# Extra node tiles and the lead of the pairs spread over the run, and the last sum moved ahead, in a graph layer on one core

## What is computed

```python
src = node_feature[edge_src]
parts = [jax.nn.relu(node_feature)]
for t in range(n_types):
    msg = jax.nn.relu(src @ W_e[t].T + b_e[t])
    msg = jnp.where((edge_type == t)[:, None], msg, jnp.zeros((), msg.dtype))
    parts.append(jax.ops.segment_sum(msg, edge_dst, num_segments=N))
agg = jnp.concatenate(parts, axis=1)
for t in range(n_types):
    o = agg @ W_n[t].T + b_n[t]
    updated = jnp.where((node_type == t)[:, None], o, updated)
# result: layernorm(x + updated + x)
```

## Time and profile before

| | us |
|---|---|
| median of three runs | 907.19 |
| profiled execution, whole | 908.36 |
| its span, first to last instruction | 906.6 |
| GpSimd busy | 674.5 (74%) |
| TensorE busy | 717.5 (79%) |
| VectorE busy | 614.0 (68%) |
| ScalarE busy | 145.8 (16%) |

### The profile page before, as it was taken

The page is one execution under the profiler, slowest core; times in us unless marked ns, Lnnn a source line. Parts: engine busy times, 40 slices in busy tenths (PEclk is TensorE's granted clock), DMA queues, the critical chain, the costliest instruction groups (busy, mean ns, idle before and its releaser), DMA issues.

```text
span 906.6 us, 13972 instructions
## 1 busy us (share of the span) xinstructions
PE 717.5 (79%) x4555; PEld 601.7 (66%) x4555; DVE 614.0 (68%) x1468; ACT 145.8 (16%) x397; POOL 674.5 (74%) x718
## 2 busy tenths in 40 slices
PE   5593066896998888888888889889887798889796
PEld 3362065785877776676677777778666677778674
DVE  6999988467676557556656666665765476757756
ACT  3293100111111101101111010111111011112120
POOL 7777777777777777777777777777777777777771
PEclk9796558799999989999999999989999898989999
DMA  8495532343543344333443344335335533434321
GB/s 251 145 313 154 138 96 77 97 111 51 146 118 105 97 109 106 96 110 90 99 122 92 94 105 113 94 94 123 95 96 128 146 69 103 110 77 121 81 53 50
DMA packets 71985, 101.39 MB, mean 112 GB/s; under 512 B 18057, under 2 KB 55437, under 8 KB 71915
## 3 DMA queue, kind: packets, MB, share of 16 engines
q0 software_dynamic: 22432, 45.99, 21.9%
q1 hardware_dynamic: 46781, 50.45, 18.7%
q10 hardware_dynamic: 2702, 4.08, 1.6%
HBM read 87.47 MB, written 12.97 MB: 111 GB/s over the span
## 4 chain that ended last, share of the span: by engine, by line
POOL 50%; PE 20%; issue 17%; DMA 6%; DVE 5%; SPq 0%; DVEq 0%; POOLq 0%
POOL tab L719 47%; DMA tab<-message_table,idx_t 5%; PE ps L1605 4%; PE ps L1687 3%; PE ps L1623 3%; POOL xg L715 3%; PE ps L1529 2%; PE ps L1680 1%; PE ps L1640 1%; DMA dst_raw<-in_dst 1%; PE ps L1636 1%; DVE h L1335 1%; PE ps L1648 1%; DVE first_wide L999 1%; PE ps L1530 1%
## 5 line engine op out<-in xcount | busy, mean ns | idle before, releaser
L719 POOL DMA_INDIRECT tab<-message_table,idx_t x630 | 595.9, 946 | 192.0 <-issue 186.8
L1605 PE MATMUL ps<-work,tab 128*128 128x126 f32 x1260 | 183.7, 289 | 111.5 <-DMA tab<-message_table,idx_t 87.3
L1217 DVE TENSOR_TENSOR work<-key_t,ps 128x378 f32<-128x378 f32 (+1 forms) x180 | 108.8, 606 | 228.9 <-PE ps L1605 226.8
L1605 PEld LDWEIGHTS ps<-work,tab 128*128 128x128 f32 x1260 | 165.3, 201 | 128.3 <-issue 84.2
L1229 DVE TENSOR_TENSOR acc<-ps,acc 128x126 f32 (+1 forms) x306 | 96.2, 314 | 30.6 <-DVE acc L1229 7.2
L1687 PE MATMUL ps<-wn_t,stage 128*128 128x384 f32 x282 | 98.6, 486 | 0.0
L715 POOL DMA_INDIRECT xg<-in_x,esrc_t x67 | 72.6, 1084 | 20.4 <-issue 17.1
L1687 PEld LDWEIGHTS ps<-wn_t,stage 128*128 128x128 f32 x282 | 53.6, 190 | 37.4
L1623 PE MATMUL ps<-first_wide,tab 128*128 128x128 f32 x450 | 65.3, 299 | 4.6 <-DVE first_wide L1293 4.6
L1623 PEld LDWEIGHTS ps<-first_wide,tab 128*128 128x128 f32 x450 | 61.5, 215 | 5.0 <-issue 5.0
L862 ACT ACTIVATE stage<-ps 128x128 f32<-128x128 f32 x47 | 13.1, 278 | 309.9 <-PE ps L1687 291.4
(11 more groups left out here) (255 smaller groups left out, 1046.7 us busy)
## 6 DMA issues: line engine op xcount, KB each, us to landing
tab<-message_table,idx_t POOLq DMA_INDIRECT x630, 3.5
message_table<-tab SPq DMA_DIRECT2D x24, 384.0 KB, 4.0
dst_raw<-dense_types SPq DMA_DIRECT2D x45, 192.0 KB
wn_raw<-message_table SPq DMA_DIRECT2D x22, 384.0 KB, 3.3
src_wide<-dense_lists SPq DMA_DIRECT2D x45, 128.0 KB, 3.3
we_raw<-early_types SPq DMA_DIRECT2D x18, 192.0 KB
be_b<-early_types SPq DMA_DIRECT2D x18, 192.0 KB
xg<-in_x SPq DMA_DIRECT2D x11, 256.0 KB, 4.0
```

What stands on the lines that cost most here:

```text
L719: pool.indirect_dma_start(msg[:, slot, :], None, table, bass.IndirectOffsetOnAxis(ap=rows, axis=0)).then_inc(signal, 16)
L1217: dve.tensor_tensor(hot[:, first:first + n, :].rearrange("p c (t w) -> p c t w", w=WIN), keys.broadcast_to((P, n, T, WIN)), iota_win.rearr ...
L1605: ins = pe.matmul(sums_bank(j, g), msg[:, column, :], hot[:, column, :], start=(c == 0), stop=(c == n - 1))
```

## The change

- The extra tiles run in ascending order and one by one: in quarters 66, 93, 127 and 146, none before the early pairs that reach it are added (`PAIR_OF`). Their loads and stores are single. Extra tiles have one transposition step (`turn_extra`, self-loops and x together) in bank 2, and their product (`LINEAR_AT`, quarters 70, 98, 130, 150) shares bank 7 with the other tiles', so each waits for the other's `finish_h`, and the next early and dense turn waits for the extra's `finish_acc`.
- Both kinds of pairs have one table of turns: each turn in the last quarter of its iteration, less one quarter for every five pairs, up to eight quarters. Before, 36 pairs stood in the last quarter of their iteration and the dense pairs behind them came every three quarters.
- A bound for each early pair (`elimit`) replaces a common one, with a new GpSimd instruction ahead of the first gather.
- Positions are read as four numbers per iteration and two or three per pair. In all the reads at L1276 go from 53 to 90; one of them is new ahead of the first quarter.
- VectorE makes the first four one-hots between the two dense lists, and TensorE waits for the node masks only ahead of the first sum.
- In the last iteration TensorE does the last sum behind one opening (L1679, L1680); the other products follow it. VectorE takes the last tiles in another order, and SyncE reads `ctl` ahead of the last two stores.

The core of the diff:

```diff
-ORDER = [NT - 1 - n for n in range(NZ)]
+ORDER = [NA + 1 + n for n in range(KE)] + [NA]
...
-LIN_PS, FIN_XT_PS = (7, 6, 2, 5), (5, 6, 5, 3)
-LAST_LIN_PS = 4
+LIN_PS, FIN_XT_PS = (7, 7, 2, 5), (5, 2, 5, 3)
+LAST_LIN_PS, LAST_FIN_XT_PS = 4, 6
...
-    return NG * min(r, LEAD_FROM) + NG - 1 + LEAD_STEP * max(r - LEAD_FROM, 0)
+    return NG * r + NG - 1 - min(LEAD, r // LEAD_EVERY)
...
-EXTRA_FROM, EXTRA_STEP = NG * (NE + 1) + 3, 6
-EXTRAS = {EXTRA_FROM + EXTRA_STEP * k: k for k in range(KE)}
+def extra_at(n):
+    ready = turn_at(PAIR_OF[n]) + E_ADD_LATER
+    r = next(r for r in range(NI) if turn_at(r) + 1 >= ready and turn_at(r) >= NG * FIRST_EXTRA)
+    return turn_at(r) + 2
+EXTRA_AT = [extra_at(n) for n in range(KE)]
+LINEAR_AT = [next(q for q in range(at + 2, at + 6) if q % NG == 2) for at in EXTRA_AT]
...
-            sp.wait_ge(fin_y[3], 1)
-            store_fin(NA - 1)
             sp.wait_ge(ctl_set, 1)
             need = sp.value_load(ctl[0:1, 0:1], min_val=0, max_val=1)
-            sp.wait_ge(fin_y[1], NZ)
-            store_fin(NA, 1, 1)
+            store_extra(KE)
+            sp.wait_ge(fin_y[3], 1)
+            store_fin(NA - 1)
...
+            pool.iota(elimit[:, :], pattern=[[0, 1]], base=LIMIT_FIRST, channel_multiplier=LIMIT_STEP,
+                      allow_small_or_imprecise_dtypes=True)
...
             def finish_acc(tile, nth, z, done):
                 dve.wait_ge(added, done)
                 dve.wait_ge(self_placed[z], nth + 1)
+                if z == 1 and nth < KE:
+                    dve.wait_ge(stage_xt[z], nth + 1)
...
+                i = early_step(q, E_ADD_LATER)
+                if i is not None:
+                    early_add(i, pair_base[SIDES])
+                    pair_base = load_bases(i + 1, NG, NG + SIDES + (i + 1 < NE))
...
             list_dense(0)
-            list_dense(1)
             dve.wait_ge(iota_moved, 1)
             dve.wait_ge(setup_copied, len(UNITS))
             for g in range(NG):
                 one_hot(0, g)
+            list_dense(1)
             unpack_dense()
             first_rows()
-            bases_of = None
+            bases_of, pair_base = None, load_bases(0, NG, PLACES)
...
-                bases_of = load_bases(j + 1, 0, PLACES if j <= NE else NG + SIDES if j < LEAD_FROM + 2 else NG)
+                bases_of = load_bases(j, 0, NG)
...
+            def turn_extra(n):
+                tile, bank = ORDER[n], fin_bank(1, n)
+                rows = min(P, N - tile * P)
+                pe.wait_ge(fin_x[1], 16 * (n + 1))
+                pe.wait_ge(self_masked[1], n + 1)
+                pe.wait_ge(d_masked, sum(turn_at(r) < EXTRA_AT[n] for r in range(NI)))
+                pe.wait_ge(e_masked, sum(turn_at(i) < EXTRA_AT[n] for i in range(NE)))
+                part = self_rows(tile)
+                for t in range(T):
+                    ins = pe.transpose(ps[:, bank, t * P:t * P + rows], part[:, t, :], ident[0:rows, 0:rows])
+                ins.then_inc(self_placed[1], 1)
+                pe.transpose(ps[:, bank, XT_AT[1]:XT_AT[1] + P], xg[:, SLOT_OF[n], :], ident[:, :]
+                             ).then_inc(fin_xt[1], 1)
...
+                extras = sum(at < turn_at(j) for at in EXTRA_AT)
+                if extras:
+                    pe.wait_ge(stage_acc[1], extras)
...
+                if behind is not None:
+                    pe.wait_ge(fin_var[1 - z], behind)
...
+                pe.wait_ge(added, ADDED["main", j, 1])
                 linear_open(KE, 1)
+                sum_group(j, 3)
                 finish_linear(Z0_TILES - 1)
-                linear_open(0, 3, first=True)
-                pe.wait_ge(added, ADDED["main", j, 1])
-                sum_group(j, 3)
-                linear_types(0, 3)
                 linear_types(KE, 1)
+                finish_linear(0, 3, first=True)
...
-            pe.wait_ge(masks_set, 1)
...
             setup_unit(KEY_UNIT, len(UNITS))
+            pe.wait_ge(masks_set, 1)
```

More of the change, by code:

```diff
@@ L554, in iteration @@
                     if j == tile + 1:
+                        before = sum(SLOT_OF[n] < tile + tiles for n in range(KE))
+                        if before:
+                            sp.wait_ge(stored[1], 16 * before)
                         sp.wait_ge(e_turned, (tile + tiles + 1) // 2)
@@ L560, in iteration @@
                         store_fin(tile, tiles)
+                for n in range(KE):
+                    if j == EXTRA_AT[n] // NG - 2:
+                        load_extra(n)
+                    if j == (LINEAR_AT[n] + 3) // NG + 1:
+                        store_extra(n)
+                if j == LOAD_LAST:
+                    load_extra(KE)
                 if j > 2 and j % 2 == 0 and j < NA:
@@ L902, in quarter @@
                     mask_selfs(ORDER[EXTRAS[q + 2]])
-                if g == 3 and 1 <= j <= NE:
-                    early_relu(j - 1)
+                if early_step(q, E_RELU_LATER) is not None:
+                    early_relu(early_step(q, E_RELU_LATER))
             def last_iteration():
@@ L1565, in early_turn @@
                     pe.wait_ge(d_masked, i)
+                extras = sum(at < turn_at(i) for at in EXTRA_AT)
+                if extras:
+                    pe.wait_ge(stage_acc[1], extras)
                 for c in range(min(2, ET - 2 * i)):
```

192 lines of the change are left out of this document (104 added, 88 removed).

## The result

The change makes the kernel slower. Four runs after it gave 976.03 to 981.25 us, median 979.02; four runs before it 906.26 to 907.55, median 907.13. The ratio is 1.079 (95% interval 1.076 to 1.082). Forecast were 904.8 us and a range of 903.4 to 906.8.

What follows compares the result with a forecast made beforehand. The GpSimd gathers were taken to pace the kernel, so only the end could gain: -2.4 us, all other terms 0, took the span from 906.6 to 904.2 us. Forecast time 904.8 us, range 903.4 to 906.8.

Steps and rivals of the forecast that it cites:

- Extra tiles and lead: Extras spread over iterations 16, 23, 31, 36 and pairs turned earlier: counted 0, delay of 7.9 us just hidden.
- the margin: Gathers' distance from waiting for a sum: 1.7 us at the start, 8.5 us in iteration 16, partly refilled each iteration.
- the extras stall the gathers: Rival, 5%: three waits of 3 us make each extra's delay 12.4 us, over the 8.5 margin; 920 us.
- The end: Behind the last gather: reordered last sum, products, tiles and stores shorten the span by 2.4 us.
- S: End of TensorE's last sum, forecast at 891.9 us (891.3 to 892.5), before at 895.0.
- TensorE's 7.4 us: Products behind the last sum: 2.74, 1.93 and 2.74 us, giving 899.3, plus 0.2 us until the last matmul drains.
- VectorE's last tile: Last node tile, forecast ready at 902.1 us instead of 903.74: 1.6 us gained.
- The two stores: SyncE's last stores, control word read ahead of them: within 0.6 us of each other, last one 0.75 us earlier.
- The cold end: Rival, 7%: TensorE's work behind the last sum runs at the slow clock; 911.9 us, half of it 908.3.
- Reads of positions, one-hots, masks, the new bound: Setup and loop terms: extra read before the first quarter hidden, the others 0; new GpSimd instruction 0 to 0.1 us.
- Hidden, with 1 us left: New read ahead of the first quarter, taken as 0.75 us, delays the group with 1.7 us of margin.

Runs made afterwards that it cites:

- lead0: The change with only the table of turns undone (pairs turn in the fourth quarter up to pair 36); 906.16 us, ratio 0.9994 to the kernel before.
- lead2: The change, but the lead stays at two quarters from pair 10 to 37 (turn in the second quarter); 974.31 us, ratio 1.077 to before.
- lead3: The change, but the lead stays at three quarters from pair 15 to 37 (turn in the first quarter); 1039.99 us, ratio 1.147 to before.
- tail_only: The kernel before with only its last iteration in the new order; 907.00 us against 908.30 before on the same chip, ratio 0.9983.
- lead2_filled15: lead2 with 15 idle identity products on TensorE ahead of the sum that waits for VectorE's adds; 939.62 us, ratio 1.036 to before.
- lead2_acc_first: lead2 with VectorE's last main-sum adds and the node tile's add ahead of the dense pair's adds and masks; 915.47 us, ratio 1.008 to before.
- lead3_tiles: lead3 with all steps of node tiles 13 to 35 one quarter later; 934.29 us, ratio 1.029 to before.
- lead2_filled: lead2 with 24 idle identity products on TensorE ahead of the sum that waits for VectorE's adds; 972.19 us, ratio 1.072 to before.

## Why the prediction was wrong

**The step that failed** is "Extra tiles and lead", in this sentence: "By the parts above this is worth nothing as long as the gathers don't stall." The condition was right and I then checked it for the extras alone, four transposes, a product and three waits. For the lead the sum has no term and gives no reason. All steps of a pair do move together, but the node tiles and the main adds do not move with them. lead0 has the extras and no lead, and costs nothing; lead2 and lead3 have a lead that stays, and cost 67 and 133 us. The missing term is per iteration: 20.4 or 22 us and more, less the 17.5 of the gathers, in each of the iterations whose pairs turn in the second or first quarter, and once some 30 us at each step from the second into the first. The order of instructions held the reason: in the first quarter VectorE's early add stands behind a tile's statistics and TensorE's turn behind a tile's product.

**What I read of the margin** did not help either: 8.5 us at iteration 16 is a distance in a loop that takes 15 us where the gathers take 17.5. It says how late one delay may be, not how long an iteration may last. The number to compare was the loop's own length with the gathers'.

**The rival "the extras stall the gathers"** had the right kind of end (stalls) with the wrong cause, and priced 15.6 us. In lead0, GpSimd's longest wait for a sum is 1.3 us, at the start, and 0.3 from 160 us on (98 to 160, then 160 to 780 us):

```profile
POOL tab L753 <- PE ps L1652: 2.5, 2, 1.3
POOL tab L753 <- PE ps L1652: 4.3, 14, 0.3
```

**The end** was right in mechanism: TensorE's products behind the last sum are the last path, and -2.4 us were forecast, 16.1 against 18.5 us profiled. That the size is met so exactly is luck, for two terms of the sum were off by nearly the same in opposite directions. S was forecast 3.8 us behind the last gather's start, and came 3.0 behind it (963.29; the landing took 2.58 us, less than any of the earlier trace rows). TensorE's 7.4 us behind it are 7.4 (963.29 to 970.7, the end of the last product less the 0.2 us that the prediction counts apart). VectorE's last tile came 11.0 us behind S, 0.8 more than forecast, with 0.55 us of it a wait for ScalarE. The two stores follow each other within 0.45 us, as forecast. Measured alone in tail_only it is 1.5 us in the ratio and 2.0 in the profiles.

**The cold end** did not occur: the granted clock is 1.00 from 945 to 970 us in the changed kernel. But the slow clock that was weighed there came at another place. I had looked for it only in the last 15 us.

**Reads of positions, one-hots, masks, the new bound**: lead0 has them all, and is within 0.1% of before. One place was not hidden in it, though. The prediction has the first groups "Hidden, with 1 us left"; the two waits at the start of lead0 (2.5 us, of which 0.6 are the usual pause) are 1.9 us of stalls, near what the end gives back. The changed kernel's trace has no stall there (at most 0.5 us to 340), so it comes in some executions and not in others, and why is open. The 90 smaller reads of the changed kernel take 752 ns in the median and at most 996, where the 53 of before took 1620 and up to 2159.

## What to carry to other kernels

Where two in-order engines hand work to each other in a loop, the steps' positions against each other are a resource like any other. Shifting one kind of work by part of an iteration removes nothing and can lengthen the loop by a half; it is free only where the loop's length was tested at each position that it passes. Before calling a shift hidden, write down, for each position, what then stands ahead of the instruction that the other engine waits for, on both engines, and compare the loop's length with the pace of what hides it, not the lateness with a margin. A wait on TensorE can also cost the slow clock behind it, as the 3.92 us in lead2 did. Idle products in the wait gave that part back; the other order, which left 1.39 us of wait, gave more.

## What the runs showed of the hardware

- Behind 3.92 us without work (lead2) TensorE ran at a granted clock of 0.50 until some 6 us later; lead2 has 25 such waits. 3.5 us of idle products in the wait (lead2_filled15) kept the clock and took 2.8 us off each iteration. Behind a wait of 1.39 us in lead2_acc_first a sum of six took 0.93 us, not 1.65.
- The same wait can be followed by either level. In lead3_tiles TensorE waits 1.81 us in iteration after iteration; in some the granted clock stays at 1.00, in others it falls some 1 us after the work has begun again (0.63 in the mean of 607 to 611 us), and the iteration takes 17.0 us instead of 15.5.
- A product of the float32 identity with itself is two matmuls in the trace of lead2_filled, 0.115 us from one to the next, not one.
